# A four-stage F32 network on one core: the second input multiplied whole instead of split in two

## The reference, cut to what matters

```python
x = _layernorm(x + _L0_attn_ref(x, ...))        # x1
x = _layernorm(x + _L0_ffn_ref(x, ...))         # x2
x = _layernorm(x + _L1_attn_ref(x, ...))        # x3
x = _layernorm(x + _L1_ffn_ref(x, ...))

# _L1_attn_ref
lifted = jnp.tanh(jax.nn.relu(x @ Wl1 + bl1) @ Wl2 + bl2)
combined = jnp.concatenate([x, lifted], axis=-1)
x_trans = jax.nn.relu(combined @ Wf1 + bf1) @ Wf2 + bf2
Bm = x_trans @ W2 + b2
Cm = x_trans @ W3 + b3
delta = jax.nn.softplus(x_trans @ W1 + b1)
dB = delta[..., :, None] * Bm[..., None, :]
dA = jnp.exp(-celu(delta[..., :, None] * A[None, None]))
h_new = dA * h_prev[:, None] + x_trans[..., None] * dB
output = jnp.einsum('bln,bldn->bld', Cm, h_new)
```

## Time and profile before

| what | value |
|---|---|
| median of three runs | 263.12 us |
| the profiled execution, its own time | 263.28 us |
| its span, first to last instruction | 261.5 us |
| mean granted clock of TensorE | 0.949 |
| PE busy | 231.7 us (89%) in 857 matmuls |
| DVE busy | 208.8 us (80%) |
| ACT busy | 183.6 us (70%) |
| POOL busy | 123.2 us (47%) |

### The profile page before, as it was taken

How to read it: one execution, slowest core, us unless ns; L and a number is a source line. 1 busy time by engine, 2 the same in 40 slices (tenths; PEclk the granted TensorE clock), 3 DMA queues, 4 the chain that set the end, 5 groups by cost and what they waited for, 6 DMA issues and landing times.

```text
span 261.5 us, 2686 instructions
## 1 busy us (share of the span) xinstructions
PE 231.7 (89%) x857; PEld 152.4 (58%) x857; DVE 208.8 (80%) x344; ACT 183.6 (70%) x249; POOL 123.2 (47%) x96
## 2 busy tenths in 40 slices
PE   7869899899999947999695999999999899999970
PEld 7869557435433323444342555578888678888850
DVE  4998793679277799996979989981599997997475
ACT  4488899969898779989998957359933643644330
POOL 3410000000027979799999965373244577055300
PEclk9997999999999975999889899999999999999995
DMA  6950000000000000000000000000000000110002
GB/s 162 373 219 1 1 0 3 0 0 0 0 0 0 0 5 1 0 0 3 1 1 0 0 0 0 3 0 0 0 0 3 0 0 0 44 40 0 1 0 80
DMA packets 4847, 6.16 MB, mean 24 GB/s; under 512 B 384, under 2 KB 2656, under 8 KB 4832
## 3 DMA queue, kind: packets, MB, share of 16 engines
q1 hardware_dynamic: 4832, 5.97, 6.8%
HBM read 4.92 MB, written 1.05 MB: 23 GB/s over the span
## 4 chain that ended last, share of the span: by engine, by line
PE 42%; DVE 23%; ACT 16%; POOL 10%; issue 7%; DMA 1%; DVEq 0%; POOLq 0%; ACTq 0%
PE ps L1360 8%; PE ps L1361 8%; PE ps L1250 7%; POOL bs L403 3%; PE ps L1148 2%; PE ps L1226 2%; PE ps L1133 2%; DVE tr L1034 2%; ACT lr_f L520 2%; POOL tr_f L395 2%; DVE xr L1031 2%; POOL bxt L382 1%; DVE tr L1031 1%; PE ps L216 1%; PE ps L1191 1%
## 5 line engine op out<-in xcount | busy, mean ns | idle before, releaser
L707 ACT ACTIVATE bs<-ps,vec 128x512 f32<-128x512 f32 x48 | 31.8, 692 | 34.7 <-PE ps L1361 33.5
L1226 PE MATMUL ps<-tr,h0sel 96*128 96x512 f32 x64 | 25.6, 512 | 11.7 <-DVE bx L941 3.8
L372 POOL CAST tr<-bs 96x512 fp32r<-96x512 f32 x4 | 2.4, 608 | 62.2 <-ACT bs L614 62.0
L1226 PEld LDWEIGHTS ps<-tr,h0sel 96*128 96x128 f32 x64 | 12.0, 205 | 24.4 <-issue 12.1
L1360 PE MATMUL ps<-xr,wf 128*128 128x512 f32 x64 | 25.4, 396 | 0.0
L1361 PE MATMUL ps<-xr,wf 128*128 128x512 f32 x64 | 25.3, 396 | 0.0
L445 POOL TENSOR_TENSOR xr<-bs,xr 128x512 fp32r<-128x512 f32 x12 | 16.1, 1349 | 14.0 <-DVE xr L1031 14.0
L445 POOL TENSOR_TENSOR tr<-bs,tr 128x512 fp32r<-128x512 f32 x8 | 10.9, 1363 | 23.0 <-DVE tr L1031 23.0
L1031 DVE CAST tr<-bs 128x512 fp32r<-128x512 f32 x16 | 7.4, 489 | 12.9 <-ACT bs L707 12.9
L445 POOL TENSOR_TENSOR x1r<-bs,x1r 128x512 fp32r<-128x512 f32 x12 | 13.8, 1155 | 8.4 <-DVE x1r L1031 8.4
L430 POOL TENSOR_TENSOR bs<-bs 128x1024 f32<-128x1024 f32 x6 | 14.3, 2385 | 3.9 <-DVE bs L947 3.8
(11 more groups left out here) (230 smaller groups left out, 685.3 us busy)
## 6 DMA issues: line engine op xcount, KB each, us to landing
wf_raw<-in_w_mlp_dram SPq DMA_DIRECT2D x2, 1024.0 KB, 8.6
bx<-in_x_dram SPq DMA_DIRECT2D x4, 256.0 KB, 5.3
out_dram<-bdl SPq DMA_DIRECT2D x4, 256.0 KB, 2.3
wf_raw<-in_w_mlp_dram SPq DMA_DIRECT2D x1, 768.0 KB, 11.3
bdl<-in_w_ssm_dram SPq DMA_DIRECT2D x1, 448.0 KB, 7.9
wa<-in_w_attn_dram SPq DMA_DIRECT2D x1, 256.0 KB, 2.7
w0raw<-in_w_ffn_dram SPq DMA_DIRECT2D x1, 192.0 KB, 7.4
h0T<-in_state_dram SPq DMA_DIRECT2D x1, 48.0 KB, 5.3
```

Source lines behind the costliest of these rows:

```text
L707: a.activation(hbuf[k][:, o, :], ring(mbank(i, stage, k, o)), ACT.Gelu if stage else ACT.Silu, scale=vec[:, s + o:s + o + 1]).then_inc(m_a ...
L1226: last = m.matmul(ps[:, 2 * j + k, :], h0sel[:, group_states(e)[j], :], tr[0:96, 0, cs(2 * (e // NG) + k)], start=True, stop=True)
```

## The change

`x2` is written once, as plain F32, into the first half of the storage of `xr` (under the name `x_f32`), and is no longer split. `layer1`, `fusion_input` and the residual's first term become one F32 product each, with the unrounded weights `w1raw` and the unrounded `centre`. Nothing reads `w1` and `centre_r` any more, so they and what makes them are gone.

```diff
-        centre_r = sb("centre_r", [P, P], F32R)
-        w1 = sb("w1", [P, 7, 2, P], F32R)
-        xr = sb("xr", [P, 2, T], F32R)
+        xr, x_f32 = sb_and_f32("xr", T)
+        x2 = x_f32[:, 0, :]
...
-            act.wait_ge(ld_w1, 16)
-            a.activation(w1[:, :, 0, :], w1raw[:, :, :], ACT.Copy).then_inc(w1_hi, 1)
...
-            v.tensor_copy(centre_r[:, :], centre[:, :]).then_inc(consts, 1)
...
-            dve.wait_ge(w1_hi, 1)
-            v.tensor_tensor(w1[:, :, 1, :], w1raw[:, :, :], full(w1[:, :, 0, :]), ALU.subtract).then_inc(w1_lo, 1)
...
             def second_input(c):
                 dve.wait_ge(y2_rs, c + 1)
-                v.tensor_tensor(bx2[:, cs(c)], ps[:, 4 + c, :], bs2[:, cs(c)], ALU.mult).then_inc(x2_ok, 1)
-                split(x2_ok, x2_hi, x2_lo, bx2, lambda c: parts(xr, c), c)
+                v.tensor_tensor(x2[:, cs(c)], ps[:, 4 + c, :], bs2[:, cs(c)], ALU.mult).then_inc(x2_ok, 1)
...
             def layer1(c):
-                wait_split(pe, x2_lo, c)
-                mm3(ps[:, 4 + c, :], pair(w1, 0), parts(xr, c)).then_inc(l1_mm, 1)
+                pe.wait_ge(x2_ok, c + 1)
+                m.matmul(ps[:, 4 + c, :], w1raw[:, 0, :], x2[:, cs(c)], start=True, stop=True).then_inc(l1_mm, 1)
...
             def fusion_input(c):
                 pe.wait_ge(l1_ok, c + 1)
-                mm3(ps[:, 4 + c, :], pair(w1, 2), parts(xr, c), stop=False)
+                m.matmul(ps[:, 4 + c, :], w1raw[:, 2, :], x2[:, cs(c)], start=True, stop=False)
...
             def state_first(c):
                 pe.wait_ge(o2_ok, c + 1)
-                for h in range(2):
-                    m.matmul(ps[:, SUM_BANK + c % 2, :], centre_r[:, :], xr[:, h, cs(c)], start=False, stop=False)
+                m.matmul(ps[:, SUM_BANK + c % 2, :], centre[:, :], x2[:, cs(c)], start=False, stop=False)
                 m.matmul(ps[:, SUM_BANK + c % 2, :], centre[:, :], bxt[:, cs(c)], start=False, stop=False)
...
-            pe.wait_ge(w1_lo, 1)
+            pe.wait_ge(ld_w1, 16)
             layer1(0)
```

More of the change, by code:

```diff
@@ L168, in build @@
                              "wqk_lo", "woT_ok")]
-        mu1_ok, w0f_ok, w0_hi, w0_lo, w1_hi, w1_lo = [
-            sem(n) for n in ("mu1_ok", "w0f_ok", "w0_hi", "w0_lo", "w1_hi", "w1_lo")]
+        mu1_ok, w0f_ok, w0_hi, w0_lo = [sem(n) for n in ("mu1_ok", "w0f_ok", "w0_hi", "w0_lo")]
         h0f_ok, h0sel_ok, h0sel_dve, a_ok = [
@@ L185, in build @@
                              "y2_var", "y2_ln", "y2_rs")]
-        x2_ok, x2_hi, l1_mm, l1_ok, l2_mm, l2_ok = [
-            sem(n) for n in ("x2_ok", "x2_hi", "l1_mm", "l1_ok", "l2_mm", "l2_ok")]
+        x2_ok, l1_mm, l1_ok, l2_mm, l2_ok = [
+            sem(n) for n in ("x2_ok", "l1_mm", "l1_ok", "l2_mm", "l2_ok")]
         f1_mm, f1_ok, xt_mm, xt_ok, d_mm, d_min, d_exp, d_ln, d_ok, d_ps = [
@@ L198, in build @@
         low_ok, low_mm, low_flag = [sem(n) for n in ("low_ok", "low_mm", "low_flag")]
-        x1_lo, x2_lo, x3_lo = [
-            sem(n) for n in ("x1_lo", "x2_lo", "x3_lo")]
+        x1_lo, x3_lo = [sem(n) for n in ("x1_lo", "x3_lo")]
         mlp_mm, m_act, m_full, m_hi, m_lo_p, m_lo_v = [
@@ L828, in _ @@
             dve.wait_ge(m_mm, 1)
-            dve.wait_ge(consts, 6)
+            dve.wait_ge(consts, 5)
             v.scalar_tensor_tensor(mix[:, :], ps[:, 2, 0:P], float(out_gain), res_centre[:, :], ALU.mult,
@@ L1156, in _ @@
             pe.wait_ge(mix_ok, 3)
-            pe.wait_ge(consts, 6)
+            pe.wait_ge(consts, 5)
             pe.wait_ge(o_ok, 1)
```

## The result

The changed kernel takes 265.19 us (median of 20 runs, 262.96 to 267.43); the kernel before, in runs beside it, 262.63 us (20 runs, 261.16 to 264.39). The ratio is 1.0085, 95% interval 1.0061 to 1.0109: 2.2 us slower, between 1.6 and 2.9. The ratio leaves out three runs of the changed kernel at 266.96 us and more, and the medians of all runs lie 2.56 us apart. In a second comparison the ratio was 1.0059, 1.0027 to 1.0090, which is 1.6 us. The forecast was +2.2 us.

The account below looks back on a forecast made before the run. The prediction took the chain to alternate between PE and ACT in the layers, with PE full from 146.2 to 175.0 us in the state stage. 1.0 + 1.2 = 2.2 us gave 265.3 us, 8-in-10 range 263.8 to 266.8.

Parts of the forecast that it names:

- c = 1: Residual's product for chunk 1 in the state stage, at 129.36 us: on the chain, +0.40 us, up to 0.86.
- DVE's and ACT's saved work: Splits of `x2`, rounding and low part of `w1`, cast of `centre_r`: covered by other waits, gain 0.
- six of eight on the path: `layer1` and `fusion_input` products in the layers: +0.17 us each, more after a wait; six count, 1.0 us in all.
- c = 0: Residual's product for chunk 0 in the state stage, near 111 us: +0.40 us on PE, hidden because ACT holds DVE.
- c = 2 and c = 3: Residual's products for chunks 2 and 3, near 145 and at 149.85 us: PE is full, +0.40 us each.
- Rival 3: State stage: one low clock stretch disappears, total +0.5 us, chance 0.07; both disappear, -1.2 us, chance 0.04.
- Rival 1: State stage: low clock makes chunks 1 and 2 cost 0.86 us each instead of 0.40; 266.2 us, chance 0.14.
- Rival 2: Start of the layers: it hangs on DVE's split, so 1.19 us comes off; 264.1 us, chance 0.08.

Follow-up runs that it names:

- dead_split: Changed kernel with the rounding of the weights and the split of `x2` done again, results unread; 264.32 us, ratio 1.0068 to the kernel before.
- layers_only: Kernel before with only the layers' products made F32, unrounded weights; residual keeps its F32R products and DVE its splits; 263.85 us, ratio 1.0035.
- double_f1b: Changed kernel with `fusion_input(1)` run twice; one run, 265.91 us.
- double_f2b: Changed kernel with `fusion_input(2)` run twice; one run, 263.30 us.
- omit_c0: Changed kernel without the residual's product of `x2` for chunk 0; one run, 263.80 us.
- omit_c23: Changed kernel without the residual's product of `x2` for chunks 2 and 3; ratio 1.0023 to the kernel before.
- state_only: Kernel before with only the residual's first term made one F32 product; layers keep `mm3` and their splits; 264.02 us, ratio 1.0037.

## Why the prediction was right

The direction, the size and the way were right: 1.0 us in the layers and 1.2 in the state stage, measured as 0.98 and 1.2 in the pair of profiles. Some of the closeness is luck. The second comparison gave 1.6 us and not 2.2. The forecast time of 265.3 lies beside the measured 265.19 although the kernel before measured 0.49 us less than when the forecast was made (262.63, then 263.12). And both profiles had the low stretch near 130, on which the term of c = 1 depends.

- *DVE's and ACT's saved work is worth nothing.* Shown by the distances in `dead_split` and, for the splits in the layers, by `layers_only`. The cover was what the prediction named: PE's F32 variance before `layer1(0)` and waits for ACT behind it; for the rounding of `w1`, the 17.9 us between ACT's table loads near 20 and 38 us are the same with and without it.
- *0.17 us for each product in the layers, six of eight on the path.* Shown by `layers_only` (+0.82 to the table load), by `double_f1b` (on the path in full) and by `double_f2b` (0.47 us of cover at `fusion_input(2)`, more than the 0.17 it needed).
- *c = 0 is hidden.* Shown by `omit_c0`.
- *c = 2 and c = 3 count in full.* The ledger gives 0.77 of 0.80. Over all profiles the way from the multiply of c = 1 to the `silu` is 40.70 and 40.78 us with the F32R products (`layers_only`, before) and 41.39 to 41.60 in those with the F32 product, the same place of c = 1 and a low stretch of 3.4 us, so the two terms are 0.6 to 0.9 us. `omit_c23` adds that DVE stands close behind, which the prediction had not looked at; it matters only to one who takes work away.
- *c = 1: +0.40.* Right in this profile (0.46), but the term is not as firm as it was put. It depends on the clock, and the moment at which the low stretch ends did not stay: the stretch moved 0.9 us with the work and kept its length of 3.4 us (128.9 to 132.4 before, 129.8 to 133.3 after). With the same length at the low clock, the added work came out at the price of full speed all the same. With the low stretch near 130, L931 to L931 takes 5.38 us (130.34 to 135.72), and 5.34 to 5.38 in the other four such profiles with the F32 product; with the two F32R calls it is 4.93 before and 4.76 in `layers_only`. So the term is 0.4 to 0.6 us there. Without it (`omit_c0`) 3.69, and 3.46 is what the step takes when nothing waits for PE. So where the low stretch near 130 is missing the term is 0.23 us at most.
- *Rival 3, the clock gives it back,* was real as a mechanism and isn't shown as an effect of the change. The stretch near 130 is missing in three of the ten profiles that leave `state_first(1)` in its place (`dead_split`, `double_f2b`, `omit_c0`) and present in seven, among them the kernel before and both of the changed one. Where it is missing, 5.38 - 3.69 = 1.7 us are saved, as that rival had priced it. It doesn't need the change: `dead_split` gives PE the same work as the changed kernel. It goes with something earlier, though. Every profile has a long low stretch near 95 to 105, and it ends at 105.0 to 106.4 us in the seven and at 107.2, 107.3 and 108.0 in the three. Here are the windows of the changed kernel and of `dead_split` (columns as in rows 8):

```profile
106.50:107.10 0.60, 0.59 (x3) 0.15 (x1) 0.60 (x2) 0.60 (x1) 0.00 (x0) 1.00 0.00 0
```

```profile
106.50:107.10 0.60, 0.60 (x2) 0.30 (x1) 0.60 (x2) 0.60 (x1) 0.06 (x1) 0.50 0.00 0
```

Counted to the end of PE's wait near 128, that is 21.7 to 23.1 us in the seven and 20.4 to 20.9 in the three. The late end itself costs nothing (the 48.67 us of `dead_split` above). The runs fit two courses: the twenty of the kernel before are ten from 261.16 to 262.31 us and ten from 262.96 to 264.39; of the changed kernel's, four lie from 262.96 to 263.91 and eleven from 265.08 to 265.61, with five elsewhere. Within the lower and within the upper groups the medians are 2.0 and 2.2 us apart, so the change costs about the same in either. The groups are drawn by eye, and whether the changed kernel falls into the upper one more often is open; too few executions have a trace.
- *Rival 1 (dearer under the low clock)* did not come: 0.46 and not 0.86 for c = 1, although its product took 1.71 us instead of 0.85. The low stretch was no longer than before, so what the product pushed out of it ran at full speed. The product of c = 2 (147.12, 0.86 us) came wholly behind the later stretch. *Rival 2 (the lighter DVE pays)* fell with `dead_split`.

## What to carry to other kernels

Splitting a value so that three F32R calls can do its product costs two elementwise instructions on another engine; whether to undo it depends on which engine has time. Here three F32R calls held TensorE 0.69 us and one F32 product 0.86, and DVE waited anyway before anything needed its work, so trading 6 us of DVE for 3 us of PE lost 2.2. Before pricing such a trade, look whether the engine that would be relieved is followed by a wait that is longer than the relief. And ask of each product on the path whether it must stand there: moving one product that nothing yet needs into a wait of PE gained 0.9 us here, in good part perhaps by keeping the low clock away. And before trusting a gain from work taken away, look how close the next engine stands: of 1.7 us removed in the full stretch about 1.0 came off.

## What the runs showed of the hardware

TensorE's clock takes different courses in executions with the same or nearly the same work of PE in front of it. The low stretch near 130 us came in seven of ten profiles, each with a wait of PE of 2.0 to 2.2 us in front of it, and 1.7 us hang on it. In these ten profiles it goes with where the long low stretch before it ended: 21.7 to 23.1 us ahead of the end of that wait in the seven, 20.4 to 20.9 in the three without.

In both kernels with `state_first(1)` moved the stretch was absent too, with the wait down to 0.90 and 0.50 us. There the earlier stretch ended 22.6 and 23.0 us ahead (104.5 to 127.06 and 105.4 to 128.40), where the other kernels had the low stretch. So the filled wait is the likelier cause, on two profiles; no run tells it from chance.

The later stretch, with a wait of 2.8 us, was there in every profile, 3.4 us long in most and 6.8 in four (the two with the move, `state_only`, `omit_c23`). In the short ones the clock fell 1.4 to 2.2 us after that wait had ended, in the long ones it fell before the wait's end or with it. One profile of a kernel is therefore good for distances between instructions within a stretch of equal clock, and not for a difference of a microsecond over the whole span.
